# A fused post-LN block: the mask's excess rows in two row tiles of 64 partitions, their products issued as pairs

## The reference

```python
attn = jnp.einsum('ds,td->st', w1, w2) * sparse_mask        # 1024 x 1024, mask: three stripes 32 apart and their transpose
y = jnp.einsum('bds,st->bdt', x, attn) + b2
x = _layernorm(x + jax.nn.gelu(y, approximate=False))
# second half: 4-bit or 8-bit bitplane weights, looked up in a table per output row
w_l = dequant_kbit(qweight, lut4, 4); w_h = dequant_kbit(qweight, lut8, 8)
y = jnp.where((norm(x) > 64)[..., None], x @ w_h.T, x @ w_l.T) + bias
x = _layernorm(x + y)
```

## Time and profile before

| | |
|---|---|
| median of 3 runs | 309.78 us (309.44 to 309.96) |
| the profiled execution | 310.19 us |
| its span in the trace | 308.4 us |
| PE busy | 292.0 us (95%), 1907 matmuls |
| DVE / ACT / POOL busy | 196.3 / 184.1 / 109.6 us |
| granted TensorE clock, mean | 0.991 of full |

### The profile page before, as it was taken

How to read it: one execution, slowest core, us unless ns; L and a number is a source line. 1 busy time by engine, 2 the same in 40 slices (tenths; PEclk the granted TensorE clock), 3 DMA queues, 4 the chain that set the end, 5 groups by cost and what they waited for, 6 DMA issues and landing times.

```text
span 308.4 us, 5056 instructions
## 1 busy us (share of the span) xinstructions
PE 292.0 (95%) x1907; PEld 255.9 (83%) x1907; DVE 196.3 (64%) x349; ACT 184.1 (60%) x244; POOL 109.6 (36%) x179
## 2 busy tenths in 40 slices
PE   7899889999999999999999999999999999999960
PEld 3788666776668999999999999999998888888860
DVE  2669898986858979798876786504134535342461
ACT  1866659787988968877896979251145443213110
POOL 4000003342443989898788200000033333333220
PEclk9999999999999999999999999999999999999996
DMA  7999999999989410110101111119147785342322
GB/s 231 397 355 356 337 348 278 245 264 219 199 146 203 100 35 34 36 36 34 36 34 37 51 48 40 53 38 299 40 143 257 252 285 200 143 170 104 123 115 80
DMA packets 28320, 49.36 MB, mean 160 GB/s; under 512 B 2432, under 2 KB 11904, under 8 KB 28288
## 3 DMA queue, kind: packets, MB, share of 16 engines
q1 hardware_dynamic: 23376, 40.36, 38.5%
q0 software_dynamic: 4352, 8.39, 15.4%
q10 hardware_dynamic: 560, 0.20, 0.2%
HBM read 36.36 MB, written 12.58 MB: 159 GB/s over the span
## 4 chain that ended last, share of the span: by engine, by line
PE 79%; DVE 9%; ACT 3%; DMA 2%; issue 2%; SPq 1%; POOL 1%; POOLq 0%; DVEq 0%; ACTq 0%
PE acc L547 19%; PE acc L549 19%; PE acc L548 19%; PE acc L530 5%; PE acc L476 5%; PE acc L420 3%; DMA w<-in_w2d 2%; PE acc L453 2%; PE acc L486 2%; PE acc L455 2%; PE acc L454 2%; PE acc L463 2%; DVE zz L1014 1%; DVE dest L972 1%; ACT z L694 1%
## 5 line engine op out<-in xcount | busy, mean ns | idle before, releaser
L547 PE MATMUL acc<-lin,zz 128*128 128x256 f32 (+2 forms) x424 | 130.2, 307 | 0.3 <-issue 0.3
L549 PE MATMUL acc<-lin,zz 128*128 128x256 f32 (+2 forms) x424 | 129.8, 306 | 0.0
L548 PE MATMUL acc<-lin,zz 128*128 128x256 f32 (+2 forms) x424 | 129.6, 306 | 0.0
L547 PEld LDWEIGHTS acc<-lin,zz 128*128 128x128 f32 x424 | 80.0, 189 | 4.6 <-issue 0.5
L548 PEld LDWEIGHTS acc<-lin,zz 128*128 128x128 f32 x424 | 80.2, 189 | 4.0
L549 PEld LDWEIGHTS acc<-lin,zz 128*128 128x128 f32 x424 | 80.1, 189 | 4.1
L712 ACT ACTIVATE leaf<-planes,lut,flip 128x1024 f32<-128x1024 uint8 x56 | 67.5, 1238 | 0.6 <-DVE dest L972 0.6
L972 DVE COPY_PREDICATED leaf<-planes,leaf 128x1024 f32<-128x1024 uint8 x32 | 43.6, 1361 | 12.4 <-ACT leaf L712 11.6
L1354 POOL DMA_DIRECT2D z<-in_xr x16 | 19.6, 1225 | 73.7 <-ACT z L694 73.7
L814 ACT ACTIVATE junk<-rows,cols 128x1024 bf16<-128x1024 f32 x15 | 17.3, 1152 | 41.7 <-POOL cols L1328 41.6
L1326 POOL TENSOR_TENSOR cols<-cols 128x1 f32<-128x1 f32 x15 | 9.5, 634 | 78.0 <-DVE rows L1089 78.0
(11 more groups left out here) (105 smaller groups left out, 437.7 us busy)
## 6 DMA issues: line engine op xcount, KB each, us to landing
z<-in_xt SPq DMA_DIRECT2D x16, 512.0 KB, 9.8
z<-in_xr POOLq DMA_DIRECT2D x16, 512.0 KB, 8.3
out_rows<-rows SPq DMA_DIRECT2D x15, 512.0 KB, 2.9
out_rows<-parts SPq DMA_DIRECT2D x32, 128.0 KB, 1.9
rows<-out_rows SPq DMA_DIRECT2D x16, 256.0 KB, 2.8
w<-in_w1d SPq DMA_DIRECT2D x7, 512.0 KB, 9.0
off_band<-in_mask_rest SPq DMA_DIRECT2D x8, 448.0 KB, 4.1
w<-in_w2d SPq DMA_DIRECT2D x3, 584.0 KB, 9.3
```

The lines of the kernel that those rows point to most:

```text
L547: nc.tensor.matmul(bank, hi, w_hi, start=k == 0, stop=False)
L548: nc.tensor.matmul(bank, hi, w_lo, start=False, stop=False)
L549: last = nc.tensor.matmul(bank, lo, w_hi, start=False, stop=k == KB - 1)
```

## The change

The excess rows are split by unit: units 0, 3, 6 go to partitions 0 to 63, units 1, 4, 7 to partitions 64 to 127. Each half has 16 rows, and they stand there four times in blocks of 16 partitions: high x with high product, high x with low product, low x with high product, and a block of zeros. A product of a unit is now a matmul of 64 partitions, and those of two units are issued one behind the other, on different halves and different banks: (0, 1), (3, 4), (6, 7). `excess(g, pair)` stands where `excess(g, units)` stood. The pair (3, 4) now comes after own 6 in full, where unit 3 came in the first place before, and the pair (6, 7) after own 7, where unit 6 came one place earlier before. Before the second and third pair PE waits for `mixed`, that is for beside 2 and beside 5, which wrote bank 3 and 6 from the other half.

`make_mix_e` is written anew: the strip's product is read twice by a broadcast (96 columns) and masked by two planes, rounded into `e_hi`, subtracted into `e_low`, and combined with a sign column (`low_sign`) into `mix_e`. `make_signs` makes the two columns on DVE at the beginning. `make_xe_lo` becomes one operation over 128 partitions. The loads grow: `w1_e` from 96 to 128 columns for each of 8 blocks (384 to 512 KB), each `xe_raw` from 96 to 128 rows (192 to 256 KB), `band_e` from 18 to 48 KB.

```diff
+def excess_order(d):
+    found = excess_rows(d)
+    units = sorted({u for u, _, _ in found})
+    return [[row for row in found if row[0] in units[tile::2]] for tile in range(2)]
...
-                sp.dma_start(xe_raw[0:EXCESS, :], xe_in[g]).then_inc(e_loaded, 16)
+                sp.dma_start(xe_raw[:, :], xe_in[g]).then_inc(e_loaded, 16)
...
-                        pe.wait_ge(mix_e_step, 4)
+                        pe.wait_ge(mix_e_step, 3)
...
-            def excess(g, units):
+            def excess(g, pair):
                 pe.wait_ge(xe_lo_made, g + 1)
                 if g == 0:
-                    pe.wait_ge(mix_e_step, 4)
-                for t in units:
-                    if t in UNITS:
-                        nc.tensor.matmul(unit_bank(t), mix_e[0:EXCESS, UNITS.index(t), :], xe[0:EXCESS, g % 2, :],
-                                         start=False, stop=False)
+                    pe.wait_ge(mix_e_step, 7)
+                if pair:
+                    pe.wait_ge(mixed, HALVES * g + halves_for([(2, 5)[pair - 1]]))
+                for tile, t in enumerate(UNITS[2 * pair:2 * pair + 2]):
+                    rows = slice(tile * SIDE, (tile + 1) * SIDE)
+                    nc.tensor.matmul(unit_bank(t), mix_e[rows, UNITS.index(t), :], xe[rows, g % 2, :],
+                                     start=False, stop=False)
...
-                excess(g, range(4))
+                excess(g, 0)
...
-                excess(g, (4, 5, 6))
+                excess(g, 1)
...
-                excess(g, (7,))
+                excess(g, 2)
...
+            def make_signs():
+                dve.wait_ge(consts_made, 4)
+                low_rows = eye.rearrange("p (a r) -> p a r", a=2)[:, :, 2 * E_ROWS:]
+                nc.vector.reduce_sum(is_low, low_rows, AXIS.XY).then_inc(mix_e_step, 1)
+                dve.wait_ge(mix_e_step, 1)
+                nc.vector.tensor_scalar(low_sign, is_low, 2.0, -1.0, ALU.mult, ALU.add).then_inc(mix_e_step, 1)
...
             def make_mix_e():
...
-                    nc.vector.tensor_copy(edges[side][0:EXCESS], raw_e[0:EXCESS, side, :, :]).then_inc(mix_e_step, 1)
-                dve.wait_ge(mix_e_step, 3)
-                rest = slice(2 * EXCESS // 3, EXCESS)
-                for side in range(2):
-                    last = nc.vector.tensor_tensor(edges[side][rest], raw_e[rest, side, :, :],
-                                                   edges[side][rest].bitcast(f32), ALU.subtract)
-                last.then_inc(mix_e_step, 1)
+                    nc.vector.scalar_tensor_tensor(edges[side], e_hi[:, 0, side, :, :].bitcast(f32), low_sign,
+                                                   e_low[:, side, :, :], ALU.mult, ALU.add).then_inc(mix_e_step, 1)
 
             def make_xe_lo(g):
                 dve.wait_ge(xe_hi_made, g + 1)
-                part = slice(EXCESS // 3, 2 * EXCESS // 3)
-                nc.vector.tensor_tensor(xe[part, g % 2, :], xe_raw[part, :], xe[part, g % 2, :].bitcast(f32),
-                                        ALU.subtract).then_inc(xe_lo_made, 1)
+                if g == 0:
+                    dve.wait_ge(mix_e_step, 1)
+                nc.vector.scalar_tensor_tensor(xe[:, g % 2, :], xe_raw[:, :], is_low, xe[:, g % 2, :].bitcast(f32), ALU.mult,
+                                               ALU.subtract).then_inc(xe_lo_made, 1)
```

More of the change, by code:

```diff
@@ L54, in post_ln_block @@
     UNITS = sorted({u for u, _, _ in excess_rows(D)})
-    EXCESS = 3 * len(excess_rows(D))
+    E_ROWS = P // 8
+    assert all(len(rows) <= E_ROWS for rows in excess_order(D))
     REST = mask_rest.shape[2]
@@ L102, in post_ln_block @@
         band = at("band", 128, [KB, P + REACH], f32)
[L103 to L106, removed]
+        w1_e = at("w1_e", 134.25, [KB, P], f32)
+        w2_e = at("w2_e", 138.25, [KB, 2 * len(UNITS) * EDGE], f32)
+        raw_e = at("raw_e", 141, [2, 2, len(UNITS), EDGE], f32)
+        band_e = at("band_e", 141.5, [2, 2, len(UNITS), EDGE], f32)
+        e_hi = at("e_hi", 142, [2, 2, len(UNITS), EDGE], f32r)
+        e_low = at("e_low", 142.5, [2, len(UNITS), EDGE], f32)
         warm = at("warm", 140, [HALF], bf16)
@@ L159, in post_ln_block @@
         off_sum = small[:, 0:KB]
-        clean, any_high, any_bad, one_col, off_total, warm_cell = (small[:, KB + n:KB + n + 1] for n in range(6))
+        clean, any_high, any_bad, one_col, off_total, warm_cell, is_low, low_sign = (small[:, KB + n:KB + n + 1] for n in range(8))
         lut_mean = energy[:, 0:KB]
@@ L295, in _ @@
             sp.dma_start(w2_e[:, :, :], w2e).then_inc(e_loaded, 16)
-            sp.dma_start(band_e[0:EXCESS, :, :, :], mask_e).then_inc(e_loaded, 16)
+            sp.dma_start(band_e[:, :, :, :, :], mask_e).then_inc(e_loaded, 16)
             load_x(0, 1)
@@ L413, in excess_strip @@
                 for d in range(KB):
-                    last = nc.tensor.matmul(unit_bank(EXCESS_BANK_UNIT)[0:EXCESS, 0:columns], w1_e[:, d, :], w2_e[:, d, :],
+                    last = nc.tensor.matmul(unit_bank(EXCESS_BANK_UNIT)[:, 0:columns], w1_e[:, d, :], w2_e[:, d, :],
                                             start=d == 0, stop=d == KB - 1)
@@ L679, in make_xe_hi @@
                     act.wait_ge(mixed, HALVES * (g - 1))
-                nc.scalar.activation(xe[0:EXCESS, g % 2, :], xe_raw[0:EXCESS, :], ACT.Copy).then_inc(xe_hi_made, 1)
+                nc.scalar.activation(xe[:, g % 2, :], xe_raw[:, :], ACT.Copy).then_inc(xe_hi_made, 1)
             def make_x_hi(g, r):
@@ L989, in make_lin_lo @@
                 if b == 0:
-                    dve.wait_ge(mix_e_step, 4)
+                    dve.wait_ge(mix_e_step, 7)
                 q, c = divmod(b, 2)
@@ L1039, in _ @@
             make_flips()
+            make_signs()
             for b in range(KB):
@@ L1440 @@
     units = sorted({u for u, _, _ in beyond})
-    rows = np.array([r for _, _, r in beyond])
-    rows_by_part = np.concatenate([rows, rows, rows])
+    e_rows = P // 8
+    in_place = [row for rows in excess_order(d) for kind in range(4) for row in (rows + rows[:1] * e_rows)[:e_rows]]
+    rows_by_part = np.array([r for _, _, r in in_place])
     edges = np.array([[P * u + (P - EDGE) * side + np.arange(EDGE) for u in units] for side in range(2)])
-    mask_e = np.zeros((len(rows), 2, len(units), EDGE), mask.dtype)
+    mask_e = np.zeros((P, 2, 2, len(units), EDGE), mask.dtype)
+    for tile, rows in enumerate(excess_order(d)):
+        for n, (u, side, r) in enumerate(rows):
+            for kind, plane in ((0, 0), (1, 1), (2, 0)):
+                place_e = P // 2 * tile + e_rows * kind + n
+                mask_e[place_e, plane, side, units.index(u)] = mask[r, edges[side, units.index(u)]]
     mask_b = np.zeros((P, kb, P + REACH), mask.dtype)
@@ L1456 @@
             mask_b[SIDE:, b, P:] = mask[last - SIDE:last, last:last + REACH]
-    for n, (u, side, r) in enumerate(beyond):
-        columns = edges[side, units.index(u)]
-        mask_e[n, side, units.index(u)] = mask[r, columns]
-        kept[r, columns] = True
+    for u, side, r in beyond:
+        kept[r, edges[side, units.index(u)]] = True
     width = int((~kept).sum(1).max())
```

18 lines of the change are left out of this document (11 added, 7 removed).

## The result

Measured side by side on one chip, the changed kernel takes 307.8 us (median of 5 runs, 306.75 to 308.22) and the kernel before 309.96 us (309.44 to 310.17). The ratio is 0.9935, 95% interval 0.9916 to 0.9953: about 2.0 us faster, between 1.5 and 2.6. The forecast was a gain of 1.4 us and a time of 308.4 us, with a range of 307.3 to 309.8.

A forecast was written before the change was run, and what follows sets the result against it. PE was taken as the bound, busy without a break from 97 us on, so earlier gains move the end. -0.20 + 0.69 + 0.69 + 0.23 = 1.41 us off 309.78 gave 308.4 us, range 307.3 to 309.8.

The forecast's parts named there:

- group 0: First group: longer DVE work and bigger loads were to eat all its saved places and cost 0.2 us, bounds 0 and 1.0.
- group 3, first place: First excess place of group 3: its 0.46 us lost in a longer wait of own(3, 4) for DVE, so no gain.
- group 3, second place: Second excess place of group 3, ahead of gelu(3, 1), which waits for PE: 0.23 us gained at the first squares.
- A pair costs one place, and the mode changes stay six: PE's excess matmuls: places 3, 2, 1 become 1, 1, 1 of 0.23 us, six full/half-row changes remain; 0.69 us a group.
- Groups 1 and 2 pass on all they gain: PE in groups 1 and 2: other engines have cover enough, so each gains 0.69 us in full.
- The rival of less: DVE later in group 1, or ACT's copies for group 2, swallow one group's gain: 0.4 to 0.9 us left; chance 0.18.
- the pairs do not run side by side: Excess pairs on PE: 24 half matmuls still need 24 places, only group 0's 0.2 loss remains, 310.0 us; chance 0.08.
- That own(0, 6) is 0.24 late: Group 0: DVE's x_lo(0, 3) ends 0.33 us later with 0.12 between it and own(0, 6)'s weights, making PE 0.24 late.
- That xe(1) lands at 47.9, at a cost of 0.2 us: End of group 0: more bytes land xe(1) at 47.9 instead of 47.1, moving own(1, 0) from 53.59 to 53.79.
- the 53.6 that the prediction took for a sign of being wrong: Start of group 1: own(1, 0) earlier than 53.6 us, or later than 54.5, would show the forecast wrong.
- The rival of more: xe(1) in time and make_mix_e no longer: group 0 costs nothing or gains, at most 2.77 us; 307.0 to 308.2; chance 0.22.
- The rival of a late xe: xe(1) lands far behind 47.9, each microsecond costing one; 1.5 us of delay brings 309.8 us; chance 0.10.

The follow-up runs named there:

- half_only: Changed kernel without the second matmul of each pair: 55.85 us from own(0, 0) to the first squares, against 55.92 for the changed kernel.
- six_g1: Changed kernel with six excess products over all 128 partitions in group 1 alone: that group takes 12.91 us, 0.68 longer.
- six_g3: Changed kernel with six full excess products in group 3 alone: 5.61 us up to own(3, 4) both times, 0.23 us lost behind it.
- z_moved: Changed kernel with the copies of z(0, 1) on ACT and DVE moved from group 2 into group 3: 307.1 us, ratio 0.9907 to the kernel before.
- from_zero: Kernel before with the DVE low parts of xe and mix_e moved to start partition 0: 57.56 us to the first squares against 57.71.
- xe_96: Changed kernel with each xe load split into transfers of 96 and 32 partitions: 56.86 us to the first squares against 55.92.
- before_128: Kernel before with each xe load filling all 128 partitions in one transfer: 57.70 us to the first squares against 57.71.

## Why the prediction was right, and where it was off

| step | forecast | measured (table) |
|---|---|---|
| group 0 | -0.20 | +0.16 |
| group 1 | +0.69 | +0.73 |
| group 2 | +0.69 | +0.70 |
| group 3, first place | 0 | -0.03 |
| group 3, second place | +0.23 | +0.23 |
| sum | 1.41 | 1.79 |

- **A pair costs one place, and the mode changes stay six.** Right: the rows of group 1, half_only, and six_g1 with 0.68. This held although no excess product of the kernel before had run as a pair; the beside pairs were the right row.
- **Group 3's first place is lost in the wait for DVE.** Right, and shown twice: by six_g3, and by z_moved, which takes copies out of the chain in front of the wait and gets the time back.
- **Groups 1 and 2 pass on all they gain.** Right: 0.73 and 0.70, and 0.68 in six_g1. The rival of less, by which DVE would be late there, did not come, nor did the one by which the pairs do not run side by side (half_only).
- **Group 0 was the term that was mis-sized, by 0.36 us of the 0.38 in the sum.** Two steps of it failed, and they make up the 0.36: 0.17 in the first, 0.19 in the second.
  - *That own(0, 6) is 0.24 late.* L464 came 0.07 late (46.59 - 36.59 against 46.34 - 36.41). The operations themselves were not cheaper than I said: 1.17 + 0.75 in place of 0.83 + 0.68 is 0.41 us, where I had 0.33 (0.27 + 0.07, so rather 0.34). But two gaps closed. `make_xe_lo` had started 0.03 behind the end of x_lo(0, 1), and now starts 0.08 before it; x_hi(0, 2) had started 0.03 behind the end of `make_mix_e`, and now starts 0.10 before it. So x_lo(0, 3) ends 0.17 later in place of 0.33. I had read durations and taken gaps as fixed. from_zero shows that these two gaps go with the start partition.
  - *That xe(1) lands at 47.9, at a cost of 0.2 us.* It landed at 45.8 and cost nothing. The price was right: xe_96 with a landing at about 48.1 loses 0.23. What failed is that I divided bytes by the rate of before; that rate was low because of the shape which the change replaces (before_128).
- **The clock times of group 0 came true by luck.** The forecast had x_lo(0, 3) ending at 46.12 and L464 at 46.58, and the profile has 46.14 and 46.59. But own(0, 0) itself started 0.18 later in this execution (36.59 against 36.41). In the same way own(1, 0) came at 53.64, just behind the 53.6 that the prediction took for a sign of being wrong. Counted from own(0, 0) it is 0.16 earlier than before, which from the start of before would be 53.46, so the sign is there.
- **The rival of more** named these very two conditions (xe(1) in time and a `make_mix_e` that gets no longer), and a part of it came: 1.79 at the squares lies above its lower end, 1.58 (309.78 - 308.2), and far below the 2.77 of all places. The measured median of 307.8 lies in its 307.0 to 308.2, too. It did not come in full, since `make_mix_e` did get longer and group 3 kept its wait.
- **The rival of a late xe** did not come in group 0. A small one came in group 3, which I had not looked at: a wait for xe(3) in some executions.
- The ratio of the runs gave 2.0 us where the profile gives 1.8 at the first squares; the interval of 1.5 to 2.6 holds both. Its lower end lies just above the 1.4 of the forecast. That group 0 was what was off is read from the stages, not from the runs.

## What to carry to other kernels

Read the gain at the first stage behind which nothing waits any more, stage by stage from a common start. Where a stage begins with a wait for another engine, places saved in front of it are worth nothing, and the work of that other engine is the next thing to move. The price of a DVE operation is its distance from start to start, and its neighbours' start partitions belong to it. Price a load by the rate of transfers of its own shape, in its own stretch: filled up to 128 partitions, xe(1) landed sooner than with 96, and xe(3) later.

## What the runs showed of the hardware

- Where the DMA busy share was 1.05 to 1.08 (34 to 38 and 42 to 46 us), the load xe(1) of 128 partitions of 2 KB landed 5.1 to 5.7 us after its issue and one of 96 after 5.9 to 6.6, at 369 to 389 against 294 to 329 GB/s in those stretches. At 62.7 us, with some 240 GB/s moved, it was the other way round for xe(3): 10.0 to 11.5 against 9.5 to 9.7 us.
- Two DVE operations began 0.07 to 0.10 us before the end of the one in front where all started at the same partition, and 0.03 us behind it where one of the two started at another (before, from_zero and after, in two places each).
- The second matmuls of the twelve pairs of 64 partitions, on the two halves of the array, cost 0.07 us in all, which is within what two executions differ by.
- The idle time that is listed before a matmul was not the pause: 0.17 us listed was 0.32 from start to start, and 0.33 came back when the wait went.
